# A long convolution by blocks of 128: three frequency streams of length 256 in place of one transform of length 1024, inside a fused decoder layer

## What is computed

```python
x = _layernorm(x + attn(x, w_q, w_k, w_v, w_o))        # 16 heads of 8, capped by tanh, causal
x = _layernorm(x + xattn(x, ctx, ...))                  # contains s4d below and a gelu MLP
x = _layernorm(x + ffn(x, ...))                         # 2 shared experts, top 2 of 8 routed

def s4d(x, log_dt, A_re, A_im, C_re, C_im, D_skip):     # x: batch, L, 128 channels
    K = 2.0 * einsum('dn,dnl->dl', dC, exp(dtA * arange(L))).real
    n = 2 * L
    y = irfft(rfft(x, n) * rfft(K, n), n)[:, :L]        # causal convolution, one filter per channel
    return y + x * D_skip
```

## Time and profile before

| | |
|---|---|
| median of 3 runs | 782.09 us |
| lowest and highest | 780.53 and 788.21 us |
| span of the profiled execution | 786.9 us |
| PE, DVE, ACT, POOL busy | 566.9, 363.1, 338.1, 251.2 us |
| mean granted PE clock | 0.824 |

### The profile page before, as it was taken

The page is one execution under the profiler, slowest core; times in us unless marked ns, Lnnn a source line. Parts: engine busy times, 40 slices in busy tenths (PEclk is TensorE's granted clock), DMA queues, the critical chain, the costliest instruction groups (busy, mean ns, idle before and its releaser), DMA issues.

```text
span 786.9 us, 10406 instructions
## 1 busy us (share of the span) xinstructions
PE 566.9 (72%) x3665; PEld 404.0 (51%) x3665; DVE 363.1 (46%) x1067; ACT 338.1 (43%) x565; POOL 251.2 (32%) x296
## 2 busy tenths in 40 slices
PE   2654552678788869878699882996987696987770
PEld 2213431455355633656436752765874675776660
DVE  4869279616673465645624571226321240133113
ACT  1186574565737556654475140330322242322220
...
DMA packets 37763, 51.60 MB, mean 66 GB/s; under 512 B 7097, under 2 KB 27362, under 8 KB 37442
## 3 DMA queue, kind: packets, MB, share of 16 engines
...
...
## 4 chain that ended last, share of the span: by engine, by line
PE 44%; DVE 23%; POOL 7%; DMA 7%; ACT 7%; issue 7%; SPq 5%; POOLq 0%; DVEq 0%; ACTq 0%
SPq L427 5%; PE ring_s L850 4%; PE bank_d L760 4%; PE bank_o L880 3%; PE bank_m L682 3%; PE ring_s L652 3%; PE ring_u L747 3%; PE bank_o L866 3%; PE ring_s L844 2%; DMA token_pairs<-y_blk,x_blk 2%; PE bank_o L669 2%; DMA x_blk<-expert_rows 2%; POOL expert_rows L1150 2%; PE bank_r L546 2%; PE ring_u L739 2%
## 5 line engine op out<-in xcount | busy, mean ns | idle before, releaser
L958 ACT ACTIVATE probs<-ring_s 128x512 f32<-128x512 f32 (+1 forms) x192 | 95.5, 524 | 118.6 <-PE ring_s L652 116.9
L1100 POOL TENSOR_SCALAR_AFFINE_SELECT probs<-probs 128x256 f32<-128x256 f32 (+1 forms) x96 | 51.6, 570 | 178.7 <-ACT probs L964 178.7
L652 PE MATMUL ring_s<-qT,kT 64*128 64x128 bf16 (+3 forms) x256 | 64.2, 350 | 49.4 <-ACT probs L958 37.8
L1013 ACT ACTIVATE g_ring<-ring_s,w_blk 128x128 f32<-128x128 f32 x184 | 52.5, 370 | 104.4 <-PE ring_s L850 95.4
...
L964 ACT ACTIVATE probs<-probs 128x2560 f32<-128x2560 f32 x32 | 74.8, 2337 | 0.8
L652 PEld LDWEIGHTS ring_s<-qT,kT 64*128 64x128 bf16 x256 | 16.4, 97 | 93.4 <-ACT probs L958 58.6
L850 PE MATMUL ring_s<-xT_blk,w_blk 128*128 128x128 f32 x368 | 57.0, 305 | 4.3 <-DVE xT_blk L1665 2.6
L682 PE MATMUL bank_m<-pair_sum,oT 128*128 128x64 f32 x256 | 44.0, 327 | 22.2 <-DVE oT L1467 22.2
L1063 POOL TENSOR_TENSOR rstd<-var_eps,neg_half 128x4 f32<-128x4 f32 x24 | 24.9, 1036 | 100.5 <-DVE var_eps L1394 100.4
L850 PEld LDWEIGHTS ring_s<-xT_blk,w_blk 128*128 128x128 f32 x368 | 53.4, 222 | 6.8 <-issue 4.3
L682 PEld LDWEIGHTS bank_m<-pair_sum,oT 128*128 128x128 f32 x256 | 39.2, 234 | 30.6 <-DVE oT L1467 25.5
...
## 6 DMA issues: line engine op xcount, KB each, us to landing
...
```

What stands on the lines that cost most here:

```text
L652: last = mm(bank[:, c:c + w], kT[64 * r:64 * r + 64, p // 2, P * j:P * (j + 1)], qT[64 * r:64 * r + 64, p, P * j:SEQ], start=True, stop=True)
L958: f(probs[:, p % 2, BASE[n]:BASE[n] + WIDTH[n]], ring_s[k % 2][:, 0:WIDTH[n]], ACT.Tanh, scale=1.0 / (CAP * float(np.sqrt(np.float32(HD))) ...
L1013: last = f(g_ring[:, s % RING, P * n:P * (n + 1)], ring_s[s % 2][:, P * n:P * (n + 1)], ACT.Gelu, bias=w_blk[:, k % SLOTS, HID + n:HID + n ...
L1100: last = g.affine_select(out=v, in_=v, compare_op=ALU.is_ge, fill=0.0, base=0, pattern=[[0, v.shape[1]], [1, P]], channel_multiplier=-1)
```

## The change

The sequence is cut in four blocks of 128 tokens, and each block, padded to 256, is transformed at 128 odd frequencies. A complex product is done with three real ones, so there are three streams: each block's transform is taken in three combinations of cosine and sine (difference, cosine, minus sine), by one 128x128 table each, moving all four blocks at once (128x512). A product of spectra becomes a sum over block lags: output block j takes input block j-m times the filter's block m, for m = 0 to 3, per stream on DVE (`lags`). `conv` adds the three streams back by three products of 128x512. For a batch PE so has 3 + 3 products of 512 columns in place of 32 + 32 of 128 columns, and DVE has 3 x 7 operations in place of 6. The filter's transform is 2 products in place of 32, with more arithmetic in `spectra`, and the tables are cut on DVE from smaller loads (`conv_tables`, run just ahead of `first_tap`). `dft` 2 waits until `lags` 0 has read its bank, since three streams share two banks.

The diff, without its renumbering:

```diff
@@ -50,7 +50,8 @@
-U_FILM, U_DFT, U_FILLS = 0, 4, 6
+NSTREAM = 3
+U_FILM, U_DFT, U_FILLS = 0, 4, 4 + NSTREAM
@@ -67,9 +68,8 @@
-    (2, 0, 0, "dft", 7), (2, 0, 1, "spectrum"), (3, 0, 5, "x2_norm"), (3, 1, 0, "x2"), (2, 1, 0, "conv", 0),
-    (2, 1, 1, "conv", 1), (2, 1, 2, "conv", 2), (2, 1, 3, "conv", 3), (2, 1, 4, "conv", 4), (2, 1, 5, "conv", 5),
-    (2, 2, 0, "conv", 6), (2, 2, 1, "conv", 7), (3, 1, 1, "x2T"), (3, 1, 3, "gates"), (1, 1, 4, "yT"),
+    (3, 0, 5, "x2_norm"), (3, 1, 0, "x2"), (2, 1, 0, "conv", 0), (2, 1, 2, "conv", 1), (2, 1, 4, "conv", 2),
+    (3, 1, 1, "x2T"), (3, 1, 3, "gates"), (1, 1, 4, "yT"),
-    (1, 6, 5, "dft", 0), (1, 7, 0, "dft", 1), (1, 7, 1, "dft", 2), (1, 7, 2, "dft", 3), (1, 7, 3, "dft", 4),
-    (1, 7, 4, "dft", 5), (1, 7, 5, "dft", 6), (2, 7, 0, "ff_out"), (2, 7, 1, "ffT"), (2, 7, 5, "ff_norm"),
+    (1, 6, 5, "dft", 0), (1, 7, 1, "dft", 1), (1, 7, 2, "lags", 0), (1, 7, 3, "dft", 2), (1, 7, 4, "lags", 1),
+    (1, 7, 5, "lags", 2), (2, 7, 0, "ff_out"), (2, 7, 1, "ffT"), (2, 7, 5, "ff_norm"),
-    (1, 1, 1, "first_tap"), *[(1, 1 + (2 + n) // NF, (2 + n) % NF, "kernel", n) for n in range(2 * NT)],
+    (1, 1, 1, "first_tap"), *[(1, 1 + (2 + n) // NF, (2 + n) % NF, "kernel", n) for n in range(2)],
...
-        cosm = sb("cosm", [P, NT, SEQ])
-        sin_fwd = sb("sin_fwd", [P, NT, SEQ])
-        sin_inv = sb("sin_inv", [P, NT, SEQ])
+        conv_tab = sb("conv_tab", [P, 2 * NSTREAM, P])
+        waves = sb("waves", [P, 2, SEQ])
+        lag_sign = sb("lag_sign", [P, 2])
-        kcn = sb("kcn", [P, NT, D])
+        taps_f = sb("taps_f", [P, NSTREAM, NT, D])
-        spec = sb("spec", [P, 2 * NT, D])
+        spec = sb("spec", [P, NSTREAM, NT, D])
...
-            for m, k in ((cosm, "c_cos"), (sin_fwd, "c_sin_fwd"), (sin_inv, "c_sin_inv")):
-                load(m[:, :, :], t[k].rearrange("(j p) f -> p j f", p=P), ld_dft)
+            load(waves[:, 0, :], t["c_cos"][0:P, :], ld_dft)
+            load(waves[:, 1, :], t["c_sin_fwd"][0:P, :], ld_dft)
+            for k, name in ((NSTREAM + 1, "c_sin_inv"), (NSTREAM + 2, "c_cos")):
+                load(conv_tab[:, k, :], t[name].rearrange("(f a) t -> f a t", a=NT)[:, 2, 0:P], ld_dft)
...
             def kernel_dft(f):
                 if f == 0:
                     pe.wait_ge(kconst_ready, 1)
-                    pe.wait_ge(ld_dft, 48)
-                mat, c = (cosm, f) if f < NT else (sin_fwd, f - NT)
-                for j in range(NT):
-                    last = mm(ring_u[f // NT][:, P * c:P * (c + 1)], mat[:, j, P * c:P * (c + 1)],
-                              kld[:, j, :], start=(j == 0), stop=(j == NT - 1))
-                if f == 2 * NT - 1:
-                    last.then_inc(pro_pe, 1)
+                mm(ring_u[f][:, :], conv_tab[:, 1 + f, :], kld.rearrange("p j d -> p (j d)"),
+                   start=True, stop=True).then_inc(pro_pe, 1)
...
             def dft(b, n):
-                f, c = divmod(n, NT)
                 if n == 0:
                     pe.wait_ge(xmod_ready, b + 1)
-                mat = (cosm, sin_fwd)[f]
-                for j in range(NT):
-                    last = mm(ring_u[f][:, P * c:P * (c + 1)], mat[:, j, P * c:P * (c + 1)], xn[:, j, :],
-                              start=(j == 0), stop=(j == NT - 1))
-                if c == NT - 1:
-                    last.then_inc(u_full, 1)
+                k = b * U_FILLS + U_DFT + n
+                pe.wait_ge(u_free, k - 1)
+                mm(ring_u[k % 2][:, :], conv_tab[:, n, :], xn[:, :, :].rearrange("p j d -> p (j d)"),
+                   start=True, stop=True).then_inc(u_full, 1)
             def conv(b, n):
-                if n == 0:
-                    pe.wait_ge(spec_ready, b + 1)
-                    if b:
-                        pe.wait_ge(ffT_sb, b)
-                j, half = divmod(n, 2)
-                for f in range(NT * half, NT * (half + 1)):
-                    mat = cosm if f < NT else sin_inv
-                    last = mm(bank_d[:, P * j:P * (j + 1)], mat[:, f % NT, P * j:P * (j + 1)], spec[:, f, :],
-                              start=(f == 0), stop=(f == 2 * NT - 1))
-                if n == 2 * NT - 1:
+                pe.wait_ge(spec_ready, NSTREAM * b + n + 1)
+                if n == 0 and b:
+                    pe.wait_ge(ffT_sb, b)
+                last = mm(bank_d[:, :], conv_tab[:, NSTREAM + n, :], spec[:, n, :, :].rearrange("p j d -> p (j d)"),
+                          start=(n == 0), stop=(n == NSTREAM - 1))
+                if n == NSTREAM - 1:
                     last.then_inc(conv_ps, 1)
...
+            def conv_tables():
+                dve.wait_ge(ld_dft, 16 * 4)
+                cos, sin = (waves[:, k, :].rearrange("p (f a) -> p f a", a=NT)[:, :, 2] for k in range(2))
+                sin_inv, cos_inv = conv_tab[:, NSTREAM + 1, :], conv_tab[:, NSTREAM + 2, :]
+                op(tt(conv_tab[:, 0, :], cos, sin, ALU.subtract))
+                op(v.tensor_copy(conv_tab[:, 1, :], cos))
+                op(ts(conv_tab[:, 2, :], sin, -1.0, None, ALU.mult))
+                op(v.tensor_copy(lag_sign[:, 0:1], waves[:, 1, 0:1]))
+                op(ts(lag_sign[:, 1:2], waves[:, 1, 0:1], -1.0, None, ALU.mult))
+                one(tt(conv_tab[:, NSTREAM, :], cos_inv, sin_inv, ALU.subtract))
+                for k in range(NSTREAM):
+                    op(ts(conv_tab[:, NSTREAM + k, :], conv_tab[:, NSTREAM + k, :], (1.0, -1.0, -1.0)[k] / P, None, ALU.mult))
+                then()
             def first_tap():
+                conv_tables()
                 dve.wait_ge(kld_landed, 16)
                 tt(kld[0:1, 0, :], kld[0:1, 0, :], dskip[:, :], ALU.add).then_inc(kconst_ready, 1)
             def spectra():
-                dve.wait_ge(pro_pe, 15)
-                op(ts(fl(kc), ring_u[0][:, :], 2.0 / (2 * SEQ), None, ALU.mult))
-                op(ts(fl(ks), ring_u[1][:, :], 2.0 / (2 * SEQ), None, ALU.mult))
-                one(ts(fl(kcn), ring_u[0][:, :], 2.0 / (2 * SEQ), None, ALU.mult))
-                op(ts(kc[0:1, 0, :], kc[0:1, 0, :], 0.5, None, ALU.mult))
-                one(ts(kcn[0:1, 0, :], ks[0:1, 0, :], 0.5, None, ALU.mult))
-                one(v.memset(ks[0:1, 0, :], 0.0))
+                dve.wait_ge(pro_pe, 16)
+                op(v.tensor_copy(fl(kc), ring_u[0][:, :]))
+                one(v.tensor_copy(fl(ks), ring_u[1][:, :]))
+                re, im, difference, total = (x[:, :, :] for x in (taps_f[:, 0], fa, taps_f[:, 1], taps_f[:, 2]))
+                op(v.tensor_copy(re[:, 0:1, :], kc[:, 0:1, :]))
+                op(v.tensor_copy(im[:, 0:1, :], ks[:, 0:1, :]))
+                op(ts(re[:, 1:NT, :], ks[:, 0:NT - 1, :], lag_sign[:, 1:2], None, ALU.mult))
+                one(ts(im[:, 1:NT, :], kc[:, 0:NT - 1, :], lag_sign[:, 0:1], None, ALU.mult))
+                op(tt(re[:, 1:NT, :], re[:, 1:NT, :], kc[:, 1:NT, :], ALU.add))
+                one(tt(im[:, 1:NT, :], im[:, 1:NT, :], ks[:, 1:NT, :], ALU.add))
+                op(tt(difference, im, re, ALU.subtract))
+                one(tt(total, im, re, ALU.add))
...
-            def spectrum(b):
-                dve.wait_ge(u_full, b * U_FILLS + U_DFT + 2)
-                re, im = ring_u[0][:, :], ring_u[1][:, :]
-                lo = spec[:, 0:NT, :].rearrange("p n d -> p (n d)")
-                hi = spec[:, NT:2 * NT, :].rearrange("p n d -> p (n d)")
-                op(tt(lo, re, fl(kc), ALU.mult))
-                op(tt(fl(xn), im, fl(ks), ALU.mult))
-                tt(hi, re, fl(ks), ALU.mult).then_inc(u_free, 1)
-                tt(fl(fb), im, fl(kcn), ALU.mult).then_inc(u_free, 1)
+            def lags(b, n):
+                k = b * U_FILLS + U_DFT + n
+                dve.wait_ge(u_full, k + 1)
+                x = ring_u[k % 2][:, :].rearrange("p (j d) -> p j d", j=NT)
+                part = (fb, kc, ks)
+                for m in range(1, NT):
+                    op(tt(part[m - 1][:, m:NT, :], x[:, 0:NT - m, :], taps_f[:, n, m:m + 1, :].broadcast_to([P, NT - m, D]), ALU.mult))
+                tt(spec[:, n, :, :], x, taps_f[:, n, 0:1, :].broadcast_to([P, NT, D]), ALU.mult).then_inc(u_free, 1)
                 then()
-                dve.wait_ge(u_free, U_FILLS * (b + 1))
-                one(tt(lo, lo, fl(xn), ALU.subtract))
-                tt(hi, hi, fl(fb), ALU.add).then_inc(spec_ready, 1)
+                dve.wait_ge(u_free, k + 1)
+                one(tt(spec[:, n, 1:NT, :], spec[:, n, 1:NT, :], fb[:, 1:NT, :], ALU.add))
+                one(tt(spec[:, n, 2:NT, :], spec[:, n, 2:NT, :], kc[:, 2:NT, :], ALU.add))
+                tt(spec[:, n, 3:NT, :], spec[:, n, 3:NT, :], ks[:, 3:NT, :], ALU.add).then_inc(spec_ready, 1)
+                dve.wait_ge(spec_ready, NSTREAM * b + n + 1)
```

More of the change, by code:

```diff
@@ L1524, in film_step @@
                 dve.wait_ge(u_full, b * U_FILLS + U_FILM + j + 1)
[L1525 removed]
+                tt(film[:, j, :], ring_u[(b * U_FILLS + U_FILM + j) % 2][:, :], film_bias[:, :], ALU.add).then_inc(u_free, 1)
```

(3 more changed lines are left out.)

9 lines of the change are left out of this document (4 added, 5 removed).

## The result

The changed kernel takes 792.7 us (median of 3 runs, 788.3 to 799.7) against 782.1: a ratio of 1.017, interval 1.010 to 1.024. In five more rounds it was 1.0165 (1.009 to 1.024). It is slower, above the forecast's range of 760 to 790, and the forecast, 777, had the wrong sign. Ratios and intervals leave out the slow executions of both kernels, those more than some 1.5% above the fastest of their kernel, and a difference of one per cent hangs on that: over all executions of the five rounds the medians were 793.4 and 786.6 us, a ratio of 1.009.

The account below looks back on a forecast made before the run. No engine was taken as the bound as a whole; each stage was read by what releases its next step. Terms +1 - 6.3 - 6.5 + 2.5 + 4 = -5.3 gave span 781.6, on the median 777 us, range 760 to 790.

Parts of the forecast that it names:

- Start, +1: Start to iteration 1, pair 3: PE's saving on the filter is lost waiting for `x_in`, then half clock: +1 us.
- some 6: Iteration 1, pair 3: PE's wait for `x_in`, landing at 193.3 as before, grows from 0.91 to some 6 us.
- `lags` at 3.1 us a step: DVE: each `lags` step takes 3.1 us, three 9.2, where `spectrum` took 4.2.
- Batch 0, -6.3: Iterations 1 and 2: pair 7 +0.2, pair 0 -2.0, pair 1 -3.4, pair 2 -1.1 us, in all -6.3.
- Batch 1, -6.5: Iterations 2 and 3: `x2T` 0.4 us earlier, fewer steps behind it -4.7, pair 2 -1.1, clock back sooner -0.3: -6.5.
- Batch 2, +2.5, end +6: Iterations 3 and 4: `ff_norm` behind `lags` delays `x2T`; +2.5 us if PE's clock returns after some 5 us, +6 if not.
- Batch 3, +4: Iterations 4 and 5: `x2T` 6.1 us late behind `lags` and `ff_norm`, partly regained by fewer steps: +4 us.
- Sum: All terms from the start to batch 3 together: -5.3 us, span 781.6.
- the second rival: PE falls to half clock in more places, work around removed steps paid double: 18.5 us more, 795; chance 0.15.

Follow-up runs that it names:

- PE work cut: Kernel before, each `dft` and `conv` step issuing 1 of its 4 products, nothing put in their place: 1.001 of the kernel before (0.996 to 1.006).
- lags cut: Changed kernel without the products for lags 1 to 3 and two additions on DVE: 0.990 of the kernel before (0.986 to 0.994).
- DVE work added: Kernel before with 7 operations of 512 columns and one of 256 per batch added on DVE behind `spectrum`: 1.034 (1.029 to 1.038).
- filler: Changed kernel with 8 unread products of 512 columns per batch added in front of PE's waits: 1.004 of the kernel before (0.998 to 1.010).

## Why the prediction was wrong

- *Start, +1.* Measured +0.4 at the head rows of iteration 1, pair 7. The mechanism was there, its parts were smaller: SP issued the load at 180.95 us for 183.06, so that PE had `x_in` at 191.54 after a wait of 2.7 us, 1.8 earlier than before and not at 193.3 again; then `qkv` ran at half clock (2.90 us for 1.54). That the sum came so near is in part luck. The wait's size, "some 6", came near in three later profiles (4.3 to 5.7).
- *`lags` at 3.1 us a step.* 3.17. Right, and `fa` stood right behind the third. The operations of 384 columns took 0.55 to 0.56 us. The Trainium skill, "VectorE: DVE Perf Modes", section on the TRN2 errata, gives 0.56 by its formula; the trace agrees.
- *Batch 0, -6.3.* Measured -2.9 by the exponential of pair 2. Two steps failed. For pair 0 I had -2.0, the removed `dft` 7; it gave 0.0. PE came out of its wait for `lags` 0 at half clock, so the product of pair 7 took 2.36 us for 1.28 and the transposes behind it 1.45 for 1.07; with a wait for ACT of 0.75 that took back what the step gave. For pair 1 I had -3.4; it lasted 11.3 us for 12.4, -1.1. I had two of the three `conv` steps at the full clock; in that pair PE was at half for most of it. After, then the product of pair 7 before:

```profile
234.58 2.07 PE L745 MATMUL ring_u<-xn,conv_tab 128*128 128x512 f32 x2 [1.83 <-DVE spec L1554]
...
236.91 2.36 PE L666 MATMUL bank_o<-probs,vv 128*32 128x512 f32 x16
...
251.09 2.36 PE L666 MATMUL bank_o<-probs,vv 128*32 128x512 f32 x16
...
253.91 2.07 PE L752 MATMUL bank_d<-spec,conv_tab 128*128 128x512 f32 x2
...
256.46 1.97 PE L679 MATMUL bank_m<-pair_sum,oT 128*128 128x64 f32 x8
...
262.36 1.28 PE L666 MATMUL bank_o<-probs,vv 128*32 128x512 f32 x16
```
```profile
236.88 1.28 PE L669 MATMUL bank_o<-probs,vv 128*32 128x512 f32 x16
```

- *Batch 1, -6.5.* Measured -6.5 by the exponential of pair 2 of iteration 3, and that is luck: two errors cancel. Apart from batch 0's gain, `x2T` came 1.4 us late and not 0.4 early, since the product of pair 7 was 2.5 late and not 0.7. From `x2T` to the product of pair 1 it took 6.1 us for 14.1, -8.0 for the -4.7 that I had from the steps, since here the clock was back and all else in that pair gained too. `x2T`'s transposes, head rows and the product that ends the pair, after, then the head rows before:

```profile
346.08 0.65 PE L548 MATMUL bank_r<-ident,x 128*128 128x128 f32 x4
346.99 1.10 PE L679 MATMUL bank_m<-pair_sum,oT 128*128 128x64 f32 x8
...
352.16 1.28 PE L666 MATMUL bank_o<-probs,vv 128*32 128x512 f32 x16
```
```profile
348.69 1.97 PE L682 MATMUL bank_m<-pair_sum,oT 128*128 128x64 f32 x8
```

- *Batch 2, +2.5, end +6.* Measured +7.7 from there to the DVE step behind `proj` (449.71 for 450.97), 0.5 of it lost in iteration 3 before pair 6. The mechanism was right and its size too (`lags`, `fa`, POOL, mask): from the end of `y_att` to the product of pair 7 it took 15.9 us, 15.6 in my walk and 7.4 before. The step that failed is the clock behind it. From the product to `x2T` it took 4.9 us for my 3.7. Behind `x2T` I let the clock return after 5 us; it stayed at half to `proj`, 11.7 us for 8.5.
- *Batch 3, +4.* Measured +4.9, `x2T` waiting 12.96 us.
- *Sum.* The terms measured give +3.6 at the first expert unit (564.28 for 560.67) for -5.3. The two terms mis-sized, 3.4 in batch 0 and 5.2 in batch 2, make 8.6 of the 8.9 between them. Most of both is PE at half clock where I had it at full, the mechanism of the second rival, to which I gave 0.15. Its sign, a mean clock below 0.78, came out in the profiled execution (0.775) but not in the second one (0.792). Its list of places did not, since in batch 1 the clock paid and didn't cost. That its time, 795, came near is in part luck: the two traces have +3.9 us, which is 786 on the median.
- *The rest.* The medians lie 10.6 us apart, the two spans 3.9. The 6.7 between are what the profiled execution of before took above its median, and which of its stages were long no trace shows. I put a difference of traces on a median; any one execution of this kernel is uncertain by that much.

So the step that failed is the price of PE's work. The forecast credited the removed steps and left most of the work around them at its old clock, while the new waits for `lags` put that work at half. "PE work cut" shows that 39 us of PE's instructions, taken out alone, are worth nothing that can be measured, and "lags cut" that with the change's products they are worth some 8 us. DVE's time I charged little beyond `ff_norm`'s row. By the ratios of "lags cut" and "DVE work added" it counts at 0.9 to 1.1 us for one, with an uncertainty of a third for the first. Where PE's waits moved is seen in the groups: without most of the `lags` it waited 2.4 us less for `oT`, 3.2 less at `x2T` and 3.7 less in `dft`; with DVE's work added 5.2 more for `oT` and 13.1 more at `x2T`. That the rest is the slower clock behind those waits is argued, not shown. That the clock has a part in it is shown (price of the same instructions before and after the waits); how much of the missing gain is the clock's and how much is the order of DVE, ACT and POOL, which set the pairs' pace once PE is shorter, stays open, since holding the clock up by filler took PE time of its own.
